# Attention probabilities turned by DMA instead of TensorE, with new order lists for every engine

## The chip, the cores and the metric

The kernel runs on one core of one Trainium2 chip. The metric is the device time of one execution in microseconds (us). Times of instructions come from one profiled execution. The engines are TensorE (PE for matmuls, PEld for its weight loads), VectorE (DVE), ScalarE (ACT), GpSimd (POOL) and SyncE (SP), whose queue here only issues DMAs.

## The reference

128 graphs of 128 nodes with 256 features. First one transformer layer (8 heads of 32), masked and biased by the adjacency matrix, then a stack of two layers of graph attention with one head:

```
nx = ln(x); q, k, v = nx@wq+bq, nx@wk+bk, nx@wv+bv                # 8 heads of 32
attn = softmax(q k^T / sqrt(32) + (0.1*adj*adj where adj > 0, else -inf))
x1 = x + (attn v)@wo + bo
x  = x1 + gelu(ln(x1)@w1+b1)@w2 + b2                              # hidden width 1024
for l in (0, 1):
    q, k = x@Wq[l].T + bq[l], x@Wk[l].T + bk[l]                   # width 128
    a = softmax(masked(q k^T / sqrt(128)))
    x = ln(x + (a x)@Wc[l].T)
```

## The kernel before

The graphs are taken in 32 groups of four (B = 4, NG = 32). A group passes through stages: N (first norm), Q (queries, keys, values), A (attention, output projection, second norm), M (the MLP), C0 and C1 (the two layers of graph attention). Each stage is cut into steps. `M.up3` is the fourth of eight chunks of the hidden layer; `A.exp2` is the exponential of the third graph's eight heads. Products in full precision are made of three float16 matmuls of high and low halves (`mm3`, lines 327 to 329), so nearly every operand is first split: ACT writes the high half, DVE or POOL the low half.

Nothing is scheduled while the kernel runs. Each engine has a list of steps written out by hand of a planner, `TENSOR`, `SCALAR`, `VECTOR`, `GPSIMD` and `SYNC`, which it goes through once in each iteration, and a second list (`..._END`) for the last. An entry as `A.exp2-1` means: in iteration n, step exp2 of stage A for group n-1. So groups overlap, five or six of them at a time, and each engine does its steps in exactly this order. Semaphores hold the engines together: `need(engine, signal, group, per, k)` waits for a count.

What the steps around the change do, for graph b of a group:

- `A.S` (PE, L1297) makes the scores of 8 heads in psA, two banks of PSUM. `A.S` on DVE (L872) scales them, adds the bias and writes `sc[:, b % 2]` (float32, in SBUF, inside the tile `area`). `A.max` (DVE, L877) takes the maxima.
- `A.exp` (ACT, L667) runs 8 exponentials over `sc`.
- `A.PT` (PE, L1304) transposes the 8 blocks of 128x128 float32 back into psA. ACT `A.PT` (L673) writes the high half of psA into `pT16`, DVE `A.PT` (L880) the low half.
- `A.AV` (PE) multiplies by v, 24 matmuls; DVE normalizes them into `o_rows`. After the fourth, `A.oT` splits `o_rows` (ACT L677 high, DVE L896 low), SP turns both halves by two DMA transposes into `rot_h`, `rot_l`; `A.wo` (PE) projects.
- DVE `A.wo` (L902) adds the residual, `A.st` (L749, L754) takes mean and variance, POOL `A.rs` (L544, L546) the inverse root, DVE `A.xh` (L762) normalizes, `A.mT` and `M.mT` split and turn again (ACT L681, DVE L913, SP), and `M.up0` to `M.up7` read the result.
- `M.up` on ACT is Gelu (L688) and a cast (L691), then DVE (even chunks) or POOL (odd chunks, L334) makes the low half, and `M.down` (PE) needs it. `psUp` is bank 3 of PSUM, and `psQ[1]`, into which `Q.q1`, `Q.k1` and `Q.v1` are made, is bank 3 too.
- Exp and Gelu need different function tables on ACT. A load of the table (`ACT_TABLE_LOAD`) stands wherever a step with Exp follows one with Gelu or the other way round; copies, casts and Identity need none.

The transposes of the other operands (xT, oT, mT, and xT of C0 and C1) are already done by SP's queue, two of 128x1024 float16 each, by `turn`:

Of the kernel before, what the change touches and what calls it, by code (L numbers as in the profile page):

```python
# [1395 lines left out]
```

## Time and profile before

| | |
|---|---|
| median of 3 runs | 2076.52 us (2076.26 to 2077.35) |
| the profiled execution | 2075.52 us |
| its span, first to last instruction | 2073.3 us |
| PE busy | 1868.7 us (90%) |
| DVE busy | 1701.3 us (82%) |
| ACT busy | 1563.1 us (75%) |
| POOL busy | 925.4 us (45%) |
| share of the 16 DMA engines, SP's queue | 38.6% |

Busy is the time in which an engine has an instruction under way. After some 110 us of filling, the kernel repeats itself once for each group until the last ones drain, so one such period shows nearly everything.

### The profile page before, as it was taken

To read this page: it belongs to the slowest core of one execution; us is meant where nothing else is said; L and a number is where in the kernel's file an instruction comes from. 1 tells how busy PE (TensorE), PEld (TensorE's weight loads), DVE (VectorE), ACT (ScalarE), POOL (GpSimd) and SP (SyncE) were. 2 spreads that over 40 slices of the span, in tenths; PEclk is the share of its full clock that TensorE was granted. 3 is DMA by queue.
4 is the path that set the end of the run, shared out by engine and by line. 5 is a ranking of instruction groups with operands and counts; after the bars stand their busy time and mean duration, and the time that the engine had idled before them with its cause. 6 is when DMAs were issued, how large, how long until landed. Compare 5 with 4: busy or idle time off the path is not lost.

```text
span 2073.3 us, 44187 instructions
## 1 busy us (share of the span) xinstructions
PE 1868.7 (90%) x15704; PEld 1347.0 (65%) x15704; DVE 1701.3 (82%) x3402; ACT 1563.1 (75%) x2996; POOL 925.4 (45%) x1168
## 2 busy tenths in 40 slices
PE   4688899999999999999999999999999999999886
PEld 3455566676666667666666766666676666666664
DVE  4766788888888888888888888888888888888756
ACT  2477677778877777887777788777778877777762
POOL 3021425555443555544355554435555443555445
PEclk8788899999999999999999999999999999999998
DMA  6212344433344443334444343444443344443212
GB/s 168 70 40 70 92 102 113 102 87 78 84 111 102 113 103 88 77 85 111 103 113 103 87 78 85 110 103 112 103 87 75 88 110 102 113 103 78 57 48 60
DMA packets 441657, 192.45 MB, mean 93 GB/s; under 512 B 347808, under 2 KB 416416, under 8 KB 441440
## 3 DMA queue, kind: packets, MB, share of 16 engines
q1 hardware_dynamic: 440416, 188.04, 38.6%
q8 instruction: 128, 2.10, 0.4%
q0 software_dynamic: 544, 0.80, 0.2%
q10 hardware_dynamic: 480, 0.79, 0.1%
q14 instruction: 89, 0.73, 0.1%
HBM read 38.55 MB, written 16.78 MB: 27 GB/s over the span
## 4 chain that ended last, share of the span: by engine, by line
PE 60%; ACT 18%; DVE 10%; POOL 5%; issue 4%; DMA 1%; SPq 1%; ACTq 0%; DVEq 0%; POOLq 0%
PE ps L327 16%; PE ps L329 16%; PE ps L328 16%; PE ps L1304 6%; ACT area L667 4%; PE ps L1366 3%; DVE st L749 2%; ACT L688 2%; DVE area L762 2%; ACT cs L709 2%; POOL hid_l L334 2%; DVE area L902 2%; ACT L709 2%; POOL rs L546 2%; POOL ve L544 2%
## 5 line engine op out<-in xcount | busy, mean ns | idle before, releaser
L544 POOL TENSOR_TENSOR ve<-mv,eps_cols 128x4 f32<-128x4 f32 x128 | 64.1, 500 | 738.5 <-DVE mv L754 738.5
L667 ACT ACTIVATE area<-area,nmax 128x128 f32<-128x128 f32 x1024 | 312.6, 390 | 17.0 <-DVE nmax L877 16.2
L327 PE MATMUL ps<-w_h,hid_h 128*128 128x256 f16 x1024 | 279.5, 273 | 12.1 <-POOL hid_l L334 12.1
L334 POOL TENSOR_TENSOR hid_l<-area,hid_h 128x512 f16<-128x512 f32 x128 | 156.4, 1222 | 279.1 <-ACT hid_h L691 279.1
L328 PE MATMUL ps<-w_l,hid_h 128*128 128x256 f16 x1024 | 279.3, 273 | 0.0
L329 PE MATMUL ps<-w_h,hid_l 128*128 128x256 f16 x1024 | 279.2, 273 | 0.0
L688 ACT ACTIVATE area<-ps,b_col 128x512 f32<-128x512 f32 x256 | 176.1, 688 | 41.0 <-PE ps L329 37.9
L327 PE MATMUL ps<-rot_h,w_h 128*128 128x512 f16 x512 | 198.5, 388 | 8.4 <-ACT area L688 5.3
L328 PE MATMUL ps<-rot_l,w_h 128*128 128x512 f16 x512 | 198.0, 387 | 0.0
L329 PE MATMUL ps<-rot_h,w_l 128*128 128x512 f16 x512 | 197.9, 387 | 0.0
L880 DVE SCALAR_TENSOR_TENSOR pT<-ps,pT 128x1024 f16<-128x1024 f32 x128 | 156.1, 1220 | 20.1 <-ACT pT L673 20.1
L551 POOL TENSOR_TENSOR x<-x,cb_row 128x256 f32<-128x256 f32 x240 | 167.3, 728 | 4.7
L858 DVE SCALAR_TENSOR_TENSOR qk<-ps,bqk_col,qk 128x512 f16<-128x512 f32 x128 | 95.6, 747 | 84.2 <-ACT qk L656 84.2
L691 ACT CAST hid_h<-area 128x512 f16<-128x512 f32 x256 | 158.2, 618 | 8.2
L872 DVE SCALAR_TENSOR_TENSOR area<-ps,biasA 128x1024 f32<-128x1024 f32 x128 | 154.9, 1211 | 5.3 <-PE ps L1297 5.3
L877 DVE TENSOR_REDUCE nmax<-area 128x8 f32<-128x1024 f32 x128 | 155.4, 1214 | 2.2
L673 ACT ACTIVATE pT<-ps 128x1024 f16<-128x1024 f32 x128 | 130.3, 1018 | 25.3 <-PE ps L1304 25.3
L1304 PE MATMUL ps<-ident,area 128*128 128x128 f32 x1024 | 138.3, 279 | 11.4 <-ACT area L667 6.7
L1366 PE MATMUL ps<-area,cs 128*128 128x256 f32 x512 | 125.2, 388 | 20.3 <-ACT cs L719 19.1
L1304 PEld LDWEIGHTS ps<-ident,area 128*128 128x128 f32 x1024 | 117.9, 144 | 33.6 <-issue 17.4
L697 ACT CAST sC_h<-area 128x1024 f16<-128x1024 f32 x32 | 33.4, 1045 | 137.8 <-DVE area L921 137.8
L546 POOL TENSOR_TENSOR rs<-ve,minus_half 128x4 f32<-128x4 f32 x128 | 132.7, 1036 | 10.0
(201 smaller groups left out, 5821.2 us busy)
## 6 DMA issues: line engine op xcount, KB each, us to landing
qkS<-qk SPq DMA_DIRECT2D x378, 128.0 KB, 2.3
xin<-in_x SPq DMA_DIRECT2D x32, 512.0 KB, 4.7
adj_in<-in_adj SPq DMA_DIRECT2D x64, 256.0 KB, 2.8
out<-x SPq DMA_DIRECT2D x30, 512.0 KB, 2.8
area<-in_L_gnn_w SPq DMA_DIRECT2D x1, 1024.0 KB, 7.9
area<-in_L_gnn_w SPq DMA_DIRECT2D x2, 512.0 KB, 9.2
rot_h<-sA_h SPq DMA_TRANSPOSE x64, 2.8
rot_l<-sA_l SPq DMA_TRANSPOSE x64, 2.7
```

Of the source, the lines that this page charges most:

```text
L327: pe.matmul(dst, lh, rh, start=start, stop=False, **kw)
L328: pe.matmul(dst, lh, rl, start=False, stop=False, **kw)
L329: return pe.matmul(dst, ll, rh, start=False, stop=stop, **kw)
L334: eng.tensor_tensor(hid_l[:, c % RING, :], hidden[:, c % 2, :], hid_h[:, c % RING, :], ALU.subtract).then_inc(done, 1)
L546: pool.tensor_tensor(rs[:, n], ve[:, n], minus_half[:, :], ALU.pow).then_inc(p_rs[n], 1)
L551: last = pool.tensor_tensor(dst[:, b], src[:, b], row, op)
L667: last = act.activation(sc[:, b % 2, h], sc[:, b % 2, h], ACT.Exp, bias=nmax[:, b, h:h + 1])
L688: act.activation(hidden[:, b % 2, :], psUp, ACT.Gelu, bias=b1_col[:, b:b + 1], scale=1.0 / W_SCALE).then_inc(a_gelu, 1)
L691: act.copy(hid_h[:, b % RING, :], hidden[:, b % 2, :]).then_inc(a_hi, 1)
L880: dve.scalar_tensor_tensor(pT16[:, b % 2, 1], psA_heads, P_SCALE, pT16[:, b % 2, 0], ALU.mult, ALU.subtract).then_inc(d_PT, 1)
L1304: last = pe.transpose(psA_heads[:, h], sc[:, b % 2, h], ident[:, :])
L1366: last = pe.matmul(rows_of(l, g)[:, b], cs[:, l, b], places(l, g)["cW"][:, b], start=True, stop=True)
```

## The change

The 8 transposes on PE are gone. ACT writes the high half of the probabilities straight from `sc` in SBUF into a new tile `sP_h`, DVE the low half into `sP_l`, both in the layout of `sc`, and SP turns each by one DMA transpose of 128x1024 float16 into `pT16`. There is one `sP_h` and one `sP_l`, so the splits of graph b wait until both transposes of graph b-1 have landed (`m_PT`). `sc[:, b % 2]` becomes free with the low half (`d_PT`) and no longer with the PE transposes. All ten order lists are new, and with them the waits on PE for banks that come free (`freed` and the `at ==` ladder). Two preparations in the first group move from `Q.mA` to `A.S0`.

```diff
+        sP_h, sP_l = sb("sP_h", [P, H, P], F16), sb("sP_l", [P, H, P], F16)
...
+                    elif what[:2] == "PT":
+                        b = int(what[2])
+
+                        need_apart(sp, t_AV, g, B, b - 1)
+                        need_apart(sp, a_PT, g, B, b + 1)
+                        sp.dma_start_transpose(pT16[:, b % 2, 0], sP_h.rearrange("p h k -> p (h k)"))\
+                            .then_inc(m_PT, 16)
+                        need_apart(sp, d_PT, g, B, b + 1)
+                        sp.dma_start_transpose(pT16[:, b % 2, 1], sP_l.rearrange("p h k -> p (h k)"))\
+                            .then_inc(m_PT, 16)
...
                     elif what[:2] == "PT" and stage == "A":
-                        need(act, t_PT, g, B, b + 1)
-                        need(act, t_AV, g, B, b - 1)
-                        act.activation(pT16[:, b % 2, 0], psA_heads, ACT.Copy, scale=P_SCALE).then_inc(a_PT, 1)
+                        need(act, a_exp, g, B, b + 1)
+                        need(act, m_PT, g, B * TURN, b * TURN)
+                        act.activation(sP_h[:, :, :], sc[:, b % 2], ACT.Copy, scale=P_SCALE).then_inc(a_PT, 1)
...
-                        need(dve, t_PT, g, B, b - 1)
+                        need(dve, d_PT, g, B, b - 1)
...
                         need(dve, a_PT, g, B, b + 1)
-                        dve.scalar_tensor_tensor(pT16[:, b % 2, 1], psA_heads, P_SCALE, pT16[:, b % 2, 0],
+                        need(dve, m_PT, g, B * TURN, b * TURN)
+                        dve.scalar_tensor_tensor(sP_l[:, :, :], sc[:, b % 2], P_SCALE, sP_h[:, :, :],
...
-                    elif stage == "A" and what[:2] == "PT":
-                        need(pe, a_exp, g, B, b + 1)
-                        for h in range(H):
-                            last = pe.transpose(psA_heads[:, h], sc[:, b % 2, h], ident[:, :])
-                        last.then_inc(t_PT, 1)
                     elif what[:2] == "AV":
-                        need(pe, d_PT, g, B, b + 1)
+                        need(pe, m_PT, g, B * TURN, (b + 1) * TURN)
```

Of the lists, the first line of ACT's before and of ACT's after:

```diff
-SCALAR = ["M.up2-2", "A.PT0-1", "M.up3-2", "A.exp1-1", "M.up4-2", "Q.k0+0", "A.PT1-1", "M.up5-2",
+SCALAR = ["M.up2-2", "A.exp1-1", "M.up3-2", "A.PT1-1", "M.up4-2", "Q.k0+0", "M.up5-2", "A.exp2-1",
```

From ACT's order in the middle of the program, before: the stretch of one iteration from `A.exp2` (L667) to `C0.ex` (L709), with `Q.q1`, `Q.k1` (L656), `C1.xT` (L697) and the high halves of graphs 2 and 3 (L673) between them.

```order
L667 ACT_TABLE_LOAD
L667 ACTIVATE area<-area,nmax 128x128 x8
L656 ACTIVATE qk<-ps,bqk_col 128x512
L697 CAST sC_h<-xh 128x1024
L673 ACTIVATE pT<-ps 128x1024
L667 ACTIVATE area<-area,nmax 128x128 x8
L656 ACTIVATE qk<-ps,bqk_col 128x512
L673 ACTIVATE pT<-ps 128x1024
L709 ACTIVATE cs,csum<-cs,cmax 128x128 x4
```

Of the changed kernel at the same place, from `A.exp3` (now L681) to `C0.ex` (L723) and on to `A.oT` (L691); the Gelu of `M.up6` is L702, its cast L705.

```order
L681 ACTIVATE area<-area,nmax 128x128 x8
L702 ACT_TABLE_LOAD
L702 ACTIVATE area<-ps,b_col 128x512
L705 CAST hid_h<-area 128x512
L687 ACTIVATE sP_h<-area 128x1024
L711 CAST sC_h<-xh 128x1024
L670 ACTIVATE qk<-ps,bqk_col 128x512
L723 ACT_TABLE_LOAD
L723 ACTIVATE cs,csum<-cs,cmax 128x128 x4
L670 ACTIVATE qk<-ps,bqk_col 128x512
L729 ACTIVATE area<-ps 128x1024
L691 CAST sA_h<-area 128x1024
```

`M.up6` stood ahead of the three exponentials and now stands among them, with a table load on either side. Over the whole program ACT has 191 table loads before and 249 after.

From SP's order, before: from the transposes of `N.xT` through the store to `C1.xT`, `A.oT` and the stacking copies `Q.stk` (L478).

```order
L429 DMA_TRANSPOSE xT_h<-sN_h 128x8x128
L432 DMA_TRANSPOSE xT_l<-sN_l 128x8x128
L496 DMA out<-x 128x4x256
L429 DMA_TRANSPOSE cT_h<-sC_h 128x8x128
L432 DMA_TRANSPOSE cT_l<-sC_l 128x8x128
L429 DMA_TRANSPOSE rot_h<-sA_h 128x8x128
L432 DMA_TRANSPOSE rot_l<-sA_l 128x8x128
L478 DMA qkS<-qk 32x2x1024 x12
```

Of the changed kernel, from the same `N.xT` on to `C1.xT`; of the pairs for graphs 0, 1 and 2 the last stands here, and the pair behind the store is graph 3's.

```order
L455 DMA_TRANSPOSE pT<-sP_h 128x8x128
L458 DMA_TRANSPOSE pT<-sP_l 128x8x128
L510 DMA out<-x 128x4x256
L455 DMA_TRANSPOSE pT<-sP_h 128x8x128
L458 DMA_TRANSPOSE pT<-sP_l 128x8x128
L433 DMA_TRANSPOSE cT_h<-sC_h 128x8x128
L436 DMA_TRANSPOSE cT_l<-sC_l 128x8x128
```

Eight transposes for each group are added to SP's queue between `N.xT` and `C1.xT`.

## Rows read from the trace of the kernel before

**Rows 1.** Stretches of one period: length, PE, PEld, DVE, ACT, POOL busy, PEclk, DMA share, GB/s.
```profile
1011.00:1054.60 43.60, 41.24 (x368) 28.83 (x366) 38.15 (x78) 41.38 (x86) 22.69 (x29) 1.00 0.25 62
1054.60:1063.40 8.80, 8.40 (x69) 7.09 (x67) 7.41 (x13) 4.16 (x5) 4.09 (x5) 1.00 0.87 178
1063.40:1071.40 8.00, 7.13 (x58) 5.25 (x57) 6.77 (x16) 2.97 (x4) 2.11 (x2) 1.00 0.76 202
sum 60.40, PE 56.77 PEld 41.17 DVE 52.33 ACT 48.51 POOL 28.88; mean PE 18.92 PEld 13.72 DVE 17.44 ACT 16.17 POOL 9.63
```

**Rows 2.** One tile, sA_h: the casts of M.mT, with their first and last start.
```profile
L681 ACT CAST sA_h<-area x32: 1044/1045/1047, 99.3 to 1975.4; 128x1024 f16<-128x1024 f32 x32
```

**Rows 3.** Waits of ACT from 1011 to 1054.6 us: total, times, longest.
```profile
ACT area L688 <- PE ps L329: 0.8, 2, 0.4
ACT pT L673 <- PE ps L1304: 0.7, 1, 0.7
ACT sA_h L677 <- DVE area L889: 0.3, 1, 0.3
```

**Rows 4.** The chain that ended last, through one period: start, duration, what.
```profile
1053.04 0.43 DVE area L889
1053.49 1.05 ACT sA_h L677
...
1057.85 1.35 POOL hid_l L334
...
1063.39 1.24 DVE area L902
...
1070.39 1.05 ACT sA_h L681
```

**Rows 5.** Groups of instructions by line: busy, mean ns; idle before.
```profile
L1304 PE MATMUL ps<-ident,area 128*128 128x128 f32 x1024 | 138.3, 279 | 11.4 <-ACT area L667 6.7 <-DVE area L872 3.8
L673 ACT ACTIVATE pT<-ps 128x1024 f16<-128x1024 f32 x128 | 130.3, 1018 | 25.3 <-PE ps L1304 25.3
L880 DVE SCALAR_TENSOR_TENSOR pT<-ps,pT 128x1024 f16<-128x1024 f32 x128 | 156.1, 1220 | 20.1 <-ACT pT L673 20.1
L853 DVE TENSOR_TENSOR sN_l<-area,sN_h 128x1024 f16<-128x1024 f32 x32 | 42.5, 1328 | 12.0 <-ACT sN_h L651 12.0
L607 ACT ACTIVATE w_h<-area 128x1024 f16<-128x1024 f32 x2 | 2.0, 1094 | 0.0
L688 ACT ACT_TABLE_LOAD x95 | 121.9, 1283 | 3.0 <-PE ps L329 1.0 <-DVE hid_l L334 0.3
```

**Rows 6.** ACT in order of time, late in the first stretch.
```profile
1043.47 0.67 ACT L656 ACTIVATE qk<-ps,bqk_col 128x512 f16<-128x512 f32 x1
1044.04 1.03 ACT L697 CAST sC_h<-xh 128x1024 f16<-128x1024 f32 x1
1044.98 1.02 ACT L673 ACTIVATE pT<-ps 128x1024 f16<-128x1024 f32 x1
1045.89 2.44 ACT L667 ACTIVATE area<-area,nmax 128x128 f32<-128x128 f32 x8
...
1050.50 0.39 ACT L709 ACTIVATE cs<-cs,cmax 128x128 f32<-128x128 f32 x1
```

**Rows 7.** The chain again: one matmul of 256 columns, one of 512.
```profile
1046.36 0.11 PE ps L327
...
1046.90 0.22 PE ps L328
```

**Rows 8.** PE in order of time: the first matmul of A.AV1 and the first behind it.
```profile
1044.61 0.18 PE L327 MATMUL ps<-v_h,pT 128*128 128x33 f16 x1
...
1045.22 0.27 PE L327 MATMUL ps<-w_h,hid_h 128*128 128x256 f16 x1
```

**Rows 9.** One tile, rot_h: SP's time to issue a transpose, and to landing.
```profile
L429 SPq DMA_TRANSPOSE rot_h<-sA_h x64: 1231/1274/1430, 83.9 to 1976.5; - x64
...
DMA to landing us min/median/max: 2.7/2.8/3.3
```

More of the change, by code:

```diff
@@ L75 @@
-QK = ("q0", "q1", "k0", "k1")
-TENSOR_END = ["M.down2-2", "C0.S-3", "A.AV0-1", "A.S3-1", "C0.xW-3", "A.PT2-1", "M.down3-2",
-              "M.up6-2", "A.AV1-1", "A.PT3-1", "A.AV2-1", "M.down4-2", "C0.PT-3", "A.AV3-1",
-              "M.up7-2", "M.down5-2", "M.down6-2", "C0.PV-3", "M.down7-2", "A.wo-1", "C1.k-4",
-              "C1.q-4", "C1.S-4", "C1.xW-4", "C1.PT-4", "M.up0-1", "C1.PV-4", "M.up1-1", "C0.q-2",
-              "M.up2-1", "M.down0-1", "M.up3-1", "C0.k-2", "M.up4-1", "M.down1-1", "C0.S-2",
-              "M.up5-1", "M.down2-1", "C0.xW-2", "M.up6-1", "M.down3-1", "C1.q-3", "C1.k-3",
-              "M.up7-1", "C1.S-3", "C0.PT-2", "M.down4-1", "M.down5-1", "C0.PV-2", "M.down6-1",
-              "C1.PT-3", "M.down7-1", "C1.xW-3", "C1.PV-3", "C0.q-1", "C0.k-1", "C0.S-1", "C0.xW-1",
-              "C0.PT-1", "C1.k-2", "C0.PV-1", "C1.q-2", "C1.S-2", "C1.xW-2", "C1.PT-2", "C1.PV-2",
-              "C1.k-1", "C1.q-1", "C1.S-1", "C1.xW-1", "C1.PT-1", "C1.PV-1"]
@@ L107 @@
-GPSIMD_END = ["C0.rs-3", "C1.rs-4", "M.lo1-1", "M.lo3-1", "C1.af-4", "M.lo5-1", "A.x1b-1",
-              "C0.af-3", "M.lo7-1", "C0.rs-2", "C1.rs-3", "C0.af-2", "C0.rs-1", "C0.af-1",
-              "C1.af-3", "C1.rs-2", "C1.af-2", "C1.af-1", "C1.rs-1"]
-SYNC_END = ["M.ldC-2", "A.oT-1", "C1.xT-4", "M.mT-1", "C0.xT-2", "C1.xT-3", "C1.sto-4", "M.ldC-1",
-            "C0.xT-1", "C1.xT-2", "C1.xT-1", "C1.sto-3", "C1.sto-2", "C1.sto-1"]
+TENSOR = ["M.up0-2", "C1.PV-5", "M.up1-2", "M.up2-2", "A.S2-1", "M.down0-2", "M.down1-2", "M.up3-2",
+          "Q.k0+0", "C0.q-3", "M.up4-2", "M.up5-2", "A.S3-1", "Q.q0+0", "C0.k-3", "M.up6-2",
+          "A.AV0-1", "M.down2-2", "C0.S-3", "A.AV1-1", "M.down3-2", "M.down4-2", "Q.q1+0",
+          "C0.xW-3", "Q.k1+0", "A.AV2-1", "M.down5-2", "A.AV3-1", "C0.PT-3", "M.up7-2", "M.down6-2",
+          "C0.PV-3", "Q.v1+0", "M.down7-2", "A.wo-1", "C1.k-4", "C1.q-4", "C1.S-4", "Q.v0+0",
+          "C1.xW-4", "A.S0+0", "A.S1+0", "C1.PT-4"]
@@ new lines @@
+QK = ("q0", "q1", "k0", "k1")
+TENSOR_END = ["M.up0-2", "C1.PV-5", "M.up1-2", "M.down0-2", "C0.k-3", "A.S2-1", "M.up2-2", "C0.q-3",
+              "M.up3-2", "A.S3-1", "M.down1-2", "C0.S-3", "M.down2-2", "A.AV0-1", "C0.xW-3",
+              "M.up4-2", "A.AV1-1", "M.down3-2", "M.up5-2", "M.up6-2", "A.AV2-1", "C0.PT-3",
+              "M.down4-2", "C1.q-4", "A.AV3-1", "M.up7-2", "M.down5-2", "C0.PV-3", "M.down6-2",
+              "M.down7-2", "C1.k-4", "A.wo-1", "C1.xW-4", "C1.S-4", "C1.k-3", "C1.PT-4", "C1.PV-4",
+              "M.up0-1", "C1.q-3", "C0.q-2", "M.up1-1", "M.down0-1", "M.up2-1", "C0.k-2", "M.up3-1",
+              "M.down1-1", "M.up4-1", "C0.S-2", "M.up5-1", "M.down2-1", "C1.S-3", "M.down3-1",
+              "M.up6-1", "C0.xW-2", "M.up7-1", "C0.PT-2", "M.down4-1", "C0.PV-2", "M.down5-1",
+              "M.down6-1", "M.down7-1", "C1.xW-3", "C1.PT-3", "C1.PV-3", "C0.q-1", "C0.k-1",
+              "C0.S-1", "C0.xW-1", "C1.k-2", "C0.PT-1", "C0.PV-1", "C1.q-2", "C1.S-2", "C1.xW-2",
+              "C1.PT-2", "C1.PV-2", "C1.k-1", "C1.q-1", "C1.S-1", "C1.xW-1", "C1.PT-1", "C1.PV-1"]
@@ new lines @@
+SCALAR_END = ["A.exp1-1", "M.up2-2", "A.PT1-1", "C0.q-3", "C0.k-3", "M.up3-2", "A.exp2-1",
[8 rows of a table added]
+VECTOR_END = ["A.max0-1", "A.S1-1", "M.mC-3", "C1.PV-5", "A.max1-1", "M.lo0-2", "A.PT0-1", "A.S2-1",
[10 rows of a table added]
+GPSIMD_END = ["C0.rs-3", "A.rs-1", "C1.rs-4", "M.lo1-1", "C1.af-4", "M.lo3-1", "M.lo5-1", "A.x1b-1",
+              "C0.af-3", "M.lo7-1", "C0.rs-2", "C1.rs-3", "C0.af-2", "C0.rs-1", "C0.af-1",
+              "C1.af-3", "C1.rs-2", "C1.af-2", "C1.rs-1", "C1.af-1"]
+SYNC_END = ["A.PT3-2", "C1.xT-5", "A.oT-2", "Q.stk-1", "M.mT-2", "M.ldC-3", "C0.xT-3", "A.PT0-1",
+            "A.PT1-1", "A.PT2-1", "C1.sto-5", "C1.xT-4", "A.PT3-1", "A.oT-1", "C1.xT-3", "M.mT-1",
+            "M.ldC-2", "C0.xT-2", "M.ldC-1", "C1.sto-4", "C0.xT-1", "C1.xT-2", "C1.xT-1",
+            "C1.sto-3", "C1.sto-2", "C1.sto-1"]
@@ L779, in prepare @@
                     prepped()
-                elif step == "Q.mA":
+                elif step == "A.S0":
                     lows(HALVES_QKV, HALVES_QKVO)
@@ L1127, in iteration @@
+                    if step == "M.up0":
                         freed(g, (d_v[1], -1, 1, 1), (a_gelu, 1, 8, 8))
```

252 lines of the change are left out of this document (125 added, 127 removed), and 51 rows, old and new, of tables (SCALAR, SCALAR_END, TENSOR, VECTOR).

## The prediction

> **What bounds the kernel now.** The page says PE 90% busy, DVE 82%, ACT 75%, and an average like that would make the PE transposes the thing to remove. So I first asked for the repeating period. The casts of M.mT start 32 times from 99.3 to 1975.4 us [rows 2], so a period is (1975.4 - 99.3) / 31 = 60.5 us. Then I followed the chain that ended last through one period. It leaves PE at two places: behind A.oT on ACT it goes over a table load, Gelu and cast of M.up7 to POOL's low half at 1057.85, then M.down7 and A.wo on PE; then DVE at 1063.39, over the norm's mean and root, and ACT again with the cast of M.mT at 1070.39 [rows 4].
>
> From that I cut the period at three events and asked for the busy time of each engine between them [rows 1]:
>
> - from the end of M.mT's cast on ACT to the end of A.oT's cast on ACT: 43.6 us, ACT busy 41.4, PE 41.2;
> - from there to the end of A.wo on PE: 8.8 us;
> - from there to the end of the next M.mT cast: 8.0 us, over DVE, POOL, DVE, ACT.
>
> These three add up to the period, 60.4 us, and they are a closed loop. The first stretch is ACT's own list, gone through in order; the other two are chains of dependent work in which neither PE's nor ACT's load matters. The reader is to see that ACT, idle 12 us in a period, is idle there almost only in the last two. In the first it waits 0.8 us for matmuls of M.up, 0.7 us for A.PT on PE and 0.3 us for the last A.AV [rows 3], together 1.8 us; the rest of the stretch is ACT instructions end to end. PE is nearly as full there, so both matter, but taking work off PE can win no more than those 1.8 us unless ACT's list gets shorter too.
>
> **The change part by part.** Per period:
>
> *PE.* Four groups of 8 transposes go. All 128 together are busy for 138 us [rows 5], 1.08 each, so PE's 56.8 us a period fall to about 52.5. On a kernel bound by PE alone this would be the gain. Here it reaches the loop only through ACT's 1.8 us.
>
> *ACT, what is the same.* Between the casts of M.mT and A.oT the new list has the same steps as the old but one: Q.v0, a cast of about 0.5 us (its neighbours of 512 columns follow each other at 0.57, from 1043.47 to 1044.04 [rows 6]), now stands ahead of M.mT, where ACT waits anyway. That takes 0.5 off the stretch.
>
> *ACT, table loads.* The old list changes between Exp and Gelu 5 times in this stretch, the new 7 times: loads ahead of C1.ex, M.up0, A.exp1, M.up3, A.exp2, M.up6 and C0.ex. One load takes 1283 ns [rows 5]. Two more are 2.6 us, and nothing hides them, because ACT has no idle time there. Over the program it is 249 loads for 191, 58 more, 74 us of ACT, which is 29 periods with two more each; the periods at the ends have fewer.
>
> *ACT, the high half.* It now reads float32 from SBUF and no longer from PSUM. From PSUM it takes 1018 ns; casts of the same size from SBUF take 1045 [rows 2], and a scaled copy from SBUF 1094 [rows 5]. So each costs between 0.03 and 0.08 us more, four of them 0.1 to 0.3; I take 0.3, since an instruction behind one from PSUM also starts early (0.91 us after it, from 1044.98 to 1045.89 [rows 6]).
>
> *DVE.* The low half takes 1220 ns from PSUM; a low half made wholly from SBUF takes up to 1328 [rows 5]. 0.4 us at most for a group, on an engine that is busy 52.3 of 60.4 us. That is hidden as long as the period stays above about 54.
>
> *DMA and SP.* Eight more transposes. SP takes 1.27 us to issue one and it lands 2.8 us from issue [rows 9], so SP is held 10.2 us more in a period. Issue by issue they stand behind N.xT and ahead of C1.xT. Pair by pair: the high half's is issued while DVE makes the low half (1.2 us), the low half's lands 2.8 us behind DVE. With one sP the next graph's split must wait 1.2 + 2.8 = 4.0 us from its cast, and between two such casts ACT now always has an exponential (2.44 us [rows 6]) and at least one M.up. For graph 3, the split stands right behind M.up6 on ACT, and A.AV3 on PE has Q.q1, C0.xW, Q.k1, A.AV2 and M.down5 ahead of it, 7 us, more than 4.0. So I cost the DMAs at nothing; if that cover were gone, each microsecond by which AV3 is late is one on the loop, since A.oT follows it. C1.xT's transposes queue behind graph 3's pair by at most 1.3 us, and C1.q is half a period away.
>
> *What is late next.* ACT's idle time in the stretch does not vanish wholly. Q.q1 writes bank 3, in which the Gelu of M.up6 reads, so the whole run from M.up6's Gelu to A.oT starts at once on both engines. On PE: Q.q1 6 x 0.22 = 1.3, C0.xW 24 x 0.11 = 2.6, Q.k1 1.3, A.AV2 0.6 [rows 8], M.down5 12 x 0.11 = 1.3, A.AV3 0.6, the last one's end a further 0.2 [rows 7], then 0.7 for DVE's reciprocal and its product (0.43 [rows 4]): 8.6 us. On ACT over the same run: cast 0.5, high half 1.0, C1.xT 0.94, Q.q1 0.57, load 1.3, C0.ex 4 x 0.39 = 1.6, Q.k1 0.57, C0.xW 0.9: 7.4 us [rows 5, 6]. ACT will wait 1.2 us for the last A.AV ahead of A.oT, where it waited 0.3. Of the 0.8 for M.up I leave 0.1, for PE has less before it. Idle: 1.3 us.
>
> *The sum.* The stretch is 43.6 - 1.8 - 0.5 + 2.6 + 0.3 + 1.3 = 45.5 us, the period 45.5 + 8.8 + 8.0 = 62.3 where it was 60.4. That is 1.9 us for each of 29 periods, 55 us. The profiled execution took 2075.5 us, so 2130.5; it is 1 us under the median of the runs shown, so 2131.
>
> For the bounds: with no idle at all and the high half at no more than before, the stretch is 43.9 and the period 0.3 us longer, 2085; with the 0.3 for the high half, 2094. With the 1.8 us of idle time all left and the 1.2 besides, the stretch is 44.2 + 3.0 = 47.2, +3.6 a period, 2180.
>
> **A rule against it.** The Trainium skill, in "ScalarE: Activation LUTs", section "Table sets: the hidden batching unit", says to batch calls by table set, and gives some 2.7 us for a load. The list of after goes against the rule. The trace agrees with the rule and not with that figure: 1283 ns [rows 5]. By the Trainium skill's figure the two loads would be 5.4 us a period and the estimate 2131 + 29 x 2.8 = 2212.
>
> **The rivals.**
>
> *PE's time comes back (10%).* If PE sets the period and ACT only follows it, the 128 transposes come off whole, 138 us, and the time is 1938. For it: PE 56.8 of 60.4 us busy, 41.2 of 43.6 in the first stretch. Against it: ACT has 41.4 there, and its list grows. It decides if ACT's stretch comes out under 43.6, which needs the two loads to fall into waiting time; I find only 1.8 + 0.5 us of that to spend against 2.9.
>
> *No change (4%).* The two effects cancel to within 0.14 us a period, 2076. This is also where it would end if the 58 loads sat in idle time and PE's relief went unused. A measurement here tells differences above about 0.2% (4 us) from none.
>
> *The transposes are late (11%).* SP issues in order. If its place in the list makes each low half wait (behind N.xT's, or for A.AV of two graphs before, whose pT16 it overwrites), A.AV3 slips and A.oT with it. For it: SP has no slack that I could read from a list, and the 16 DMA engines are 76 to 87% busy in the last two stretches [rows 1]. Against it: the first stretch, where most of the new ones fall, has 25%. Price: 1.5 us a period would be 44 us on top, 2175.
>
> *A DMA transpose at its price for one block (1%).* If a DMA turned its 8 blocks of 128x128 one after another at more than PE's whole A.PT each, the ring would need over 60 us a period for eight of them and set the time, far above 2200. The trace has 2.8 us for all 8 [rows 9], which nearly rules it out. The Trainium skill, "VectorE: DVE Perf Modes", section "The three transpose paths", has 1309 ns for a 128x128 block by DMA and 390 by TensorE and advises TensorE where PSUM is a possible destination. By it an estimate is 8 x 8 x 1.3 = 84 us a period and some 2760 us.
>
> **How the numbers follow.** The forecast, slower by the table loads, has 74%. Its own range is 2094 to 2150 for most of it. To hold the time 8 times in 10 I take 2088 (near the lower bound) to 2168 (part of the late transposes); the faster rival stays outside. Faster by over 0.2% 10%, within 0.2% 4%, slower 86% (74 + 11 + 1).
>
> **What the profile of after would show.** Right: a period near 62.3 us; ACT busy near 51 us in it and 43 to 44 of the stretch from M.mT's to A.oT's cast; 7 loads there at 1283 ns; PE busy about 52.5 a period with idle time where it now has none; a wait of about 1 us of the cast of A.oT for DVE; the other two stretches still 8.8 and 8.0. The first step is wrong if the stretch between the casts is under 43.6 us. The DMA step is wrong if PE's A.AV waits for pT. The forecast fails too if the granted clock of PE, 1.00 in all three stretches now, falls as PE idles more.

## The result

The kernel after takes 2168.41 us, median of 3 runs (2164.00 to 2172.01), where the kernel before takes 2076.52: 92 us more, a ratio of 1.0442 with a 95% interval of 1.0425 to 1.0458. The forecast was slower, at 2131 with a range of 2088 to 2168, and the measured time lies 0.4 us above its top. The sign came out as forecast, the size did not: 92 us against 55. How much of the forecast's mechanism stands is told below: two loops turned out to be nearly equally long.

The page of after, its engines and the groups of instructions that answer to [rows 5]. The columns are line, engine, operation, tiles, then busy us, mean ns of one, and the idle time before them with what ended it:

```profile
PE 1823.7 (84%) x14680; PEld 1245.6 (58%) x14680; DVE 1720.8 (79%) x3402; ACT 1641.3 (76%) x3054; POOL 1032.0 (48%) x1168
...
L338 POOL TENSOR_TENSOR hid_l<-area,hid_h 128x512 f16<-128x512 f32 x128 | 175.2, 1368 | 369.0 <-ACT hid_h L705 369.0
...
L895 DVE SCALAR_TENSOR_TENSOR sP_l<-area,sP_h 128x1024 f16<-128x1024 f32 x128 | 174.6, 1364 | 35.3 <-ACT sP_h L687 35.2
...
L702 ACT ACT_TABLE_LOAD x124 | 159.1, 1283 | 3.2 <-PE ps L333 1.0
...
L687 ACT ACTIVATE sP_h<-area 128x1024 f16<-128x1024 f32 x128 | 134.5, 1050 | 16.7 <-DMA pT<-sP_l 16.5
...
pT<-sP_h SPq DMA_TRANSPOSE x128, 2.7
pT<-sP_l SPq DMA_TRANSPOSE x128, 2.7
```

The reader is to see four things. PE has lost its transposes and is at 84% where it was at 90. ACT has 124 loads ahead of Gelu where it had 95 [rows 5]. The transposes land 2.7 us from issue, close to the 2.8 costed (a median; the longest of the low halves takes 4.9). And two groups are dearer than before though the same work: the low half on DVE, 1364 ns for 1220, and POOL's low half of hidden, 1368 ns for 1222 on the page of before.

The casts of M.mT in after, which answer to [rows 2]:

```profile
L695 ACT CAST sA_h<-area x32: 1044/1045/1046, 105.6 to 2075.6; 128x1024 f16<-128x1024 f32 x32
```

(2075.6 - 105.6) / 31 is a period of 63.55 us where it was 60.52: 3.03 us in each of 31 periods, 94 us, which is the whole loss. The same three stretches as in [rows 1] follow for a period of after that ACT's waits lengthen, and behind it the first stretch of a short period. Columns: stretch, length, then busy us of PE, PEld, DVE, ACT and POOL with their instructions, PEclk, DMA share, GB/s:

```profile
1060.13:1107.44 47.31, 39.95 (x338) 25.40 (x337) 40.34 (x72) 43.48 (x86) 25.38 (x27) 0.96 0.47 112
1107.44:1116.01 8.57, 8.49 (x69) 7.16 (x68) 6.63 (x18) 4.56 (x6) 5.07 (x7) 1.00 0.85 159
1116.01:1124.05 8.04, 7.21 (x54) 5.29 (x53) 6.78 (x16) 3.15 (x5) 2.10 (x2) 1.00 0.64 163
sum 63.92, PE 55.65 PEld 37.85 DVE 53.75 ACT 51.19 POOL 32.54; mean PE 18.55 PEld 12.62 DVE 17.92 ACT 17.06 POOL 10.85
...
997.62:1043.53 45.91, 39.39 (x338) 25.81 (x336) 38.82 (x72) 43.51 (x86) 25.18 (x27) 0.96 0.57 116
```

The second and third stretches are what they were. The first holds 43.5 us of ACT work, 2.1 more than before, in the short period as in the long one. It is 45.9 us long at its best, 0.4 above the 45.5 of the forecast, and 47.3 in the period shown. What fills the difference is waiting, ACT's waits in the long one (total, times, longest), which answer to [rows 3]:

```profile
ACT sA_h L691 <- DVE area L904: 1.3, 1, 1.3
ACT area L702 <- POOL hid_l L338: 1.1, 1, 1.1
ACT sP_h L687 <- DMA pT<-sP_l: 1.0, 1, 1.0
```

The first of them was forecast at 1.2. The other two were not: a Gelu that waits for POOL's low half two chunks before it, since the Gelu overwrites the half of `hidden` that POOL still reads, and a high half of the split that waits until the transposes of the graph before have left the one sP. Over 27 such periods the means are 1.5 us ahead of A.oT, 0.8 for POOL, 0.4 for sP and 0.2 for M.up, 3.0 us in all with the smallest ones, where the forecast had 1.3.

The last of the three waits is the rival of the late transposes in small. The chain that ended last goes over it in this period (start, duration, what):

```profile
1092.24 0.04 PE ps L333
...
1092.44 1.23 SPq L455
...
1093.78 4.24 DMA pT<-sP_l
...
1098.10 1.07 ACT sP_h L687
```

SP issues graph 2's pair only behind A.AV0 on PE, whose half of `pT16` it overwrites, and here the low half's transpose takes 4.24 us to land; then ACT goes on with graph 3's split.

The granted clock is at its lower level about once in each period. In the long period above it falls here, PE in order of time and then three windows around it:

```profile
1085.93 0.39 PE L331 MATMUL ps<-xT_h,wqk_h 128*128 128x512 f16 x1 [1.98 <-DVE qk L872]
1086.15 0.46 PE L332 MATMUL ps<-xT_l,wqk_h 128*128 128x512 f16 x1
1086.40 0.63 PE L333 MATMUL ps<-xT_h,wqk_l 128*128 128x512 f16 x1
```

```profile
1083.90:1085.90 2.00, 0.05 (x1) 0.00 (x0) 1.91 (x3) 1.49 (x3) 0.34 (x1) 1.00 0.58 131
1086.40:1089.70 3.30, 3.30 (x9) 1.22 (x8) 2.49 (x5) 3.29 (x10) 2.46 (x4) 0.50 0.02 5
1089.80:1093.10 3.30, 3.30 (x43) 2.25 (x42) 2.65 (x4) 3.30 (x8) 3.22 (x4) 1.00 0.01 2
```

PE has stood still for 1.98 us ahead of Q.q0, waiting for DVE's Q.k0. It starts again, and from 1086.4 to 1089.7 its clock is 0.50, the 1.2 GHz level: a matmul of 512 columns takes 0.43 us from start to start (1086.40 to 1086.83) where [rows 7] have 0.22. In other periods it falls behind a wait of 1.60 us ahead of A.S1. Before, the clock was 1.00 in all three stretches [rows 1].

### The profile page after: what moved, and what is told of

It is laid out like the page before. It is cut to its first block, busy times and chain, and to the rows that moved or that the text cites. A ratio compares the mean times of both kernels' runs of the same rounds, so it can differ in the third digit from the quotient of the medians.

```text
span 2166.3 us, 42837 instructions
## 1 busy us (share of the span) xinstructions
PE 1823.7 (84%) x14680; PEld 1245.6 (58%) x14680; DVE 1720.8 (79%) x3402; ACT 1641.3 (76%) x3054; POOL 1032.0 (48%) x1168
## 3 DMA queue, kind: packets, MB, share of 16 engines
q1 hardware_dynamic: 710752, 255.18, 52.5%
## 4 chain that ended last, share of the span: by engine, by line
PE 33%; DVE 29%; ACT 16%; issue 9%; POOL 7%; DMA 5%; SPq 1%; DVEq 0%; ACTq 0%; POOLq 0%
PE ps L331 11%; PE ps L333 10%; PE ps L332 10%; DVE st L763 4%; DVE area L776 3%; DMA pT<-sP_l 3%; DVE area L886 3%; POOL hid_l L338 3%; ACT area L702 3%; DVE sP_l L895 3%; DVE nmax L891 3%; ACT area L681 3%; POOL rs L560 2%; ACT L702 2%; DVE x L970 2%
## 5 line engine op out<-in xcount | busy, mean ns | idle before, releaser
L338 POOL TENSOR_TENSOR hid_l<-area,hid_h 128x512 f16<-128x512 f32 x128 | 175.2, 1368 | 369.0 <-ACT hid_h L705 369.0
L681 ACT ACTIVATE area<-area,nmax 128x128 f32<-128x128 f32 x1024 | 312.5, 390 | 16.6 <-DVE nmax L891 15.8
L331 PE MATMUL ps<-rot_h,w_h 128*128 128x512 f16 x512 | 208.4, 407 | 60.5 <-ACT area L702 57.4
L702 ACT ACTIVATE area<-ps,b_col 128x512 f32<-128x512 f32 x256 | 175.9, 687 | 46.5 <-PE ps L333 23.8
L332 PE MATMUL ps<-rot_l,w_h 128*128 128x512 f16 x512 | 206.7, 404 | 0.0
L895 DVE SCALAR_TENSOR_TENSOR sP_l<-area,sP_h 128x1024 f16<-128x1024 f32 x128 | 174.6, 1364 | 35.3 <-ACT sP_h L687 35.2
L565 POOL TENSOR_TENSOR x<-x,cb_row 128x256 f32<-128x256 f32 x240 | 195.3, 844 | 4.7
L886 DVE SCALAR_TENSOR_TENSOR area<-ps,biasA 128x1024 f32<-128x1024 f32 x128 | 155.5, 1215 | 44.1 <-PE ps L1324 37.2
L565 POOL TENSOR_TENSOR x<-xh,cg_row 128x256 f32<-128x256 f32 x120 | 140.1, 1196 | 80.1 <-DMA out<-x 80.1
L331 PE MATMUL ps<-xT_h,wqk_h 128*128 128x512 f16 x256 | 102.3, 400 | 81.2 <-DVE qk L872 78.5
L705 ACT CAST hid_h<-area 128x512 f16<-128x512 f32 x256 | 158.2, 618 | 8.4
L702 ACT ACT_TABLE_LOAD x124 | 159.1, 1283 | 3.2 <-PE ps L333 1.0
L1324 PE MATMUL ps<-qkS 96*128 96x128 f16 x1024 | 83.2, 227 | 82.6 <-DVE area L886 60.7
L687 ACT ACTIVATE sP_h<-area 128x1024 f16<-128x1024 f32 x128 | 134.5, 1050 | 16.7 <-DMA pT<-sP_l 16.5
L331 PEld LDWEIGHTS ps<-rot_h,w_h 128*128 128x128 f16 x512 | 52.3, 102 | 152.4 <-ACT area L702 106.6
```

The costliest lines, as they stand in the source:

```text
L331: pe.matmul(dst, lh, rh, start=start, stop=False, **kw)
L332: pe.matmul(dst, lh, rl, start=False, stop=False, **kw)
L338: eng.tensor_tensor(hid_l[:, c % RING, :], hidden[:, c % 2, :], hid_h[:, c % RING, :], ALU.subtract).then_inc(done, 1)
L565: last = pool.tensor_tensor(dst[:, b], src[:, b], row, op)
L681: last = act.activation(sc[:, b % 2, h], sc[:, b % 2, h], ACT.Exp, bias=nmax[:, b, h:h + 1])
L687: act.activation(sP_h[:, :, :], sc[:, b % 2], ACT.Copy, scale=P_SCALE).then_inc(a_PT, 1)
```

## The experiments

All periods below are cut as above, and the means are over the same 27 periods of a run, without the first and last ones. "Low clock" is the time per period in which the records show the 1.2 GHz level. Stretch 1 runs from the cast of M.mT to that of A.oT.

| kernel | time, us | period | stretch 1 | ACT busy in it | low clock |
|---|---|---|---|---|---|
| before | 2076.5 | 60.5 | 43.5 | 41.3 | 0.0 |
| after | 2168.4 | 63.6 | 46.9 | 43.5 | 3.9 |
| e1 transposes by DMA, old lists | 2423.7 | 72.2 | 54.0 | 41.3 | 11.4 |
| e12 the same, A.PT3 first on SP | 2206.3 | 64.5 | 47.5 | 41.3 | 4.3 |
| e15 the same, two sP | 2200.3 | 64.4 | 47.4 | 41.2 | 3.3 |
| e2 before, no Gelu | 2055.1 | 60.1 | 43.3 | 35.0 | 0.5 |
| e3 after, no Gelu | 2136.5 | 62.7 | 46.4 | 34.5 | 3.7 |
| e4 before, two more loads | 2168.4 | 63.5 | 46.5 | 44.0 | 0.8 |
| e5 after, PE filled | 2153.2 | 63.1 | 46.4 | 43.4 | 0.3 |
| e13 the same, four hidden | 2140.5 | 62.6 | 45.9 | 43.4 | 0.1 |
| e6 after, two sP | 2165.0 | 63.6 | 46.9 | 43.5 | 4.0 |
| e7 after, Q.k0 earlier | 2205.2 | 64.9 | 48.3 | 43.6 | 5.3 |
| e9 the same, PE filled | 2162.9 | 63.5 | 46.9 | 43.4 | 0.4 |
| e8 e7 without Gelu | 2104.4 | 61.5 | 45.1 | 34.4 | 3.3 |
| e10 e9 without Gelu | 2103.7 | 61.6 | 45.1 | 34.4 | 0.0 |
| e11 after, five loads | 2291.2 | 67.7 | 51.0 | 41.1 | 8.2 |
| e14 the same, two sP, four hidden, PE filled in two places | 2276.7 | 67.2 | 50.6 | 41.1 | 5.8 |

e2, e3, e4, e8, e10, e12, e14 and e15 are single runs; their differences below a few us are not read.

**The transposes alone.** The DMA transposes went into the kernel before, its lists for ACT, DVE and POOL kept, A.PT taken out of PE's and put into SP's:

```diff
-SYNC = ["C1.xT-4", "A.oT-1", "Q.stk+0", "M.ldC-2", "N.ld+1", "M.mT-1", "C0.xT-2", "Q.ldA+1",
-        "N.xT+1", "C1.sto-4"]
+SYNC = ["C1.xT-4", "A.PT3-1", "A.oT-1", "Q.stk+0", "M.ldC-2", "N.ld+1", "M.mT-1", "C0.xT-2", "Q.ldA+1",
+        "N.xT+1", "A.PT0+0", "A.PT1+0", "C1.sto-4", "A.PT2+0"]
```

> The splits in SBUF and the DMA transposes of the changed kernel, but with the order lists of before: A.PT taken out of PE's list and put into SP's (graphs 0, 1 and 2 behind N.xT, graph 3 ahead of A.oT), nothing else moved, 191 table loads as before. If ACT's list with its two more table loads is what made the change slower, the DMA path by itself costs nearly nothing: ACT's stretch from M.mT to A.oT keeps its 41.8 us of work, gains 0.3 for reading SBUF, loses the 0.7 us wait for PE's transposes; period 60.0 to 60.6 us, time 2060 to 2085 us. If the DMA path itself (late transposes, POOL slowed by DVE's reads of SBUF, the clock) is the cause, most of the 92 us comes back here: 2130 us or more. If PE were the bound, its 138 us would come off: about 1940 us.

Measured: 2423.7 us (2423.51 to 2425.12), ratio 1.168 (1.1661 to 1.17). Had ACT's list been the whole cause, the time would have been at most 2085; it is 340 us above that, in the range of the rival (the DMA path itself, 2130 or more). PE's waits over one period, from 1025 to 1097 us:

```profile
PE ps L328 <- DMA pT<-sP_l: 10.6, 2, 7.2
```

A.AV stands still twice a period for the low half's transpose, 10.6 us in all. SP's queue over that place, in order of time (each row is one issue):

```profile
1067.31 1.25 SPq L452 DMA_TRANSPOSE pT<-sP_h  x1
1068.66 1.24 SPq L455 DMA_TRANSPOSE pT<-sP_l  x1
1076.75 1.23 SPq L430 DMA_TRANSPOSE cT_h<-sC_h  x1
1078.09 1.24 SPq L433 DMA_TRANSPOSE cT_l<-sC_l  x1
1079.52 1.23 SPq L452 DMA_TRANSPOSE pT<-sP_h  x1
```

Between graph 2's pair and graph 3's stands C1.xT, and SP waits 6.8 us before it may issue that. A later run swaps the two names:

```diff
-SYNC = ["C1.xT-4", "A.PT3-1", "A.oT-1", "Q.stk+0", "M.ldC-2", "N.ld+1", "M.mT-1", "C0.xT-2", "Q.ldA+1",
+SYNC = ["A.PT3-1", "C1.xT-4", "A.oT-1", "Q.stk+0", "M.ldC-2", "N.ld+1", "M.mT-1", "C0.xT-2", "Q.ldA+1",
```

> DMA transposes with the lists of before (2424 us), and on SP's queue A.PT3 ahead of C1.xT. If C1.xT's place on SP made A.AV3 late, its wait of 5.3 us falls by 2.5 (two issues) and the time to 2340 to 2360. If it is the distance from exp to A.AV in the old lists of ACT and PE that is short, nothing changes: 2400 to 2430.

Measured: 2206.3 us, 217 less, far more than the two issues that I had priced; both theories missed. The low clock fell with it, from 11.4 to 4.3 us a period, so the 217 are the swap and what follows from it. PE's waits over one period of it, from 1015.3 to 1079.6 us:

```profile
PE ps L328 <- DMA pT<-sP_l: 3.5, 1, 3.5
```

What stands ahead in SP's queue had cost its own waiting time, 6.8 us, besides two issues. With that mended the old lists, with their five loads, still lose 4.0 us a period. So the new lists as a whole do buy something: 0.9 us a period, two loads paid included. A second buffer of the split was given to this kernel as well:

> DMA transposes with the old lists, A.PT3 ahead of C1.xT on SP (2206 us, period 64.5, ACT waiting 1.4 for the DMA of the split before and 1.2 and 2.6 for PE behind it), and with two buffers of sP. If the reuse of sP delays the whole run: 1.4 us a period less, 2160 to 2170. If PE's A.AV waits for the transposes anyway: within 10 us of 2206.

2200.3 us: within the 10 us of the rival. ACT's wait for sP is gone (1.4 us a period to nothing), its wait for PE behind it is 3.7 us where it was 2.6. PE's A.AV waits the same 3.5 us.

**The table loads.** Two loads more in before, by an Exp of 4 columns ahead of M.up6's Gelu, everything else unchanged:

```diff
+                        if what == "up6":
+                            act.activation(tiny[:, :], minus_half[:, :], ACT.Exp)
```

> The kernel before with one Exp of 4 elements on ACT between M.up5 and M.up6: two more table loads a period (251 for 191), no other change, PE's transposes still in. Theory of ACT's list: each load is on the loop, 2.6 us and 0.3 for the small instruction, 2.9 us for each of 29 periods, 84 us: about 2160 us. If PE sets the period, the loads take ACT's idle time: under 2100 us.

2168.4 us. This was forecast within 10 us. Two loads in that stretch cost the kernel before 3.0 us a period: 2.7 more of ACT's work, the small Exp included, and 0.2 more of waiting for M.up. That it is also the time of after is a coincidence: there the loads are one term beside others, a cast less in the stretch, longer waits and the clock. Then the loads were taken out of both kernels, by Identity in place of Gelu:

> The kernel before with Identity in place of Gelu, so that ACT never changes its table (1 load for 191); this leaves out the Gelu. Theory of ACT's list: 5 loads leave the first stretch and 1 the second, 7.7 us of the 60.4 us period, until PE (56.8 us busy) holds it: period 57 to 58 us, 1970 to 2010 us.

> The changed kernel with Identity in place of Gelu (1 load for 249); this leaves out the Gelu. Theory of ACT's list: 8 loads go, 10.3 us of the 63.6 us period, until PE (52.5) or DVE (about 54) holds it: period 55 to 57 us, 1910 to 1970 us, so that the changed kernel is now the faster of the two. If the DMA path itself is the cause, it stays slower than the kernel before without loads by much of the 92 us: 2050 us or more.

2055.1 and 2136.5 us. The theory of ACT's list missed both by 45 us or more, in the same way: 6.3 and 9.0 us of ACT work left stretch 1, and it became 0.2 and 0.6 us shorter. The price of a load is one-sided in these kernels. A load added costs in full, a load taken away gives nearly nothing, so another engine's list is as long as ACT's.

The two runs say more, and it bears on the forecast. Without any load the changed kernel is still 81 us slower than the old one (2136.5 against 2055.1), which is the range that the second expectation gave to its rival (2050 or more). Of the 92 us no more than 32 go away with all the loads. So the two new loads are not the loss by themselves; in after the other loop alone, its low clock included, holds 62.7 us a period.

**Which list that is.** In after, PE's run to A.AV3 begins with Q.q0, and Q.q0 waits for Q.k0 on DVE (the 1.98 us above). In this kernel Q.k0 goes ahead of A.S3 on DVE:

```diff
-          "A.PT1-1", "A.S3-1", "Q.k0+0", "C1.xh-5", "M.lo4-2", "A.max3-1", "Q.q0+0", "A.PT2-1",
+          "A.PT1-1", "Q.k0+0", "A.S3-1", "C1.xh-5", "M.lo4-2", "A.max3-1", "Q.q0+0", "A.PT2-1",
```

> The changed kernel with one swap in DVE's list: Q.k0 ahead of A.S3. PE's Q.q0 waits 2.0 us for Q.k0's low half to leave bank 2, and DVE itself waits 0.75 us for PE's A.S3 ahead of it. With Gelu left out the changed kernel still took 2136 us, so a second loop, DVE's list from M.mT to Q.k0 and then PE's list from Q.q0 to A.AV3, is nearly as long as ACT's. If both loops are about equally long, shortening this one by up to 2 us gives back only the difference to ACT's: 0.3 to 1.2 us a period, 2133 to 2160 us. If this loop alone sets the period: 1.9 us a period, about 2112 us. If ACT's alone: no change.

> The same swap with Identity in place of Gelu (this leaves out the Gelu), so that both loops are shorter. If the loop over DVE and PE is what holds the changed kernel without loads at 62.7 us a period, the swap takes 1.5 to 2 us off each: 2075 to 2095 us, where the one without the swap took 2136. If something else holds it, the time stays near 2136 us.

2205.2 us with Gelu (2194.31 to 2205.89, ratio 1.0613, 1.0587 to 1.0638), 37 slower than after. All three theories missed: they had 8 to 35 faster, 56 faster, and no change. Without Gelu 2104.4, 32 faster than e3 where 41 to 61 were expected. The low clock rose to 5.3 us a period, and the periods without any were 62.52 to 62.54 us, as long as the best of after. To tell the swap from the clock, both were run with PE kept busy (the edit is that of e5, below):

> The kernel after with Q.k0 ahead of A.S3 on DVE, as in the run before this one, and with dummy matmuls of PE in the three places where it idles (ahead of A.S1, C1.PT and Q.q0). Theory: the loss of that swap, 2205 against 2168 us, was the clock alone, since its periods without a stretch at the lower level were 62.5 us; with PE kept busy all periods are 62.5 and the time is 2135 to 2153. Rival: the swap itself is late for A.S3 and so for the exponentials; then the time stays above 2165.

> The kernel of the run before with Identity in place of Gelu (the Gelu is left out), so that no table is loaded; 2104 us without the dummy matmuls. Theory of a second loop (DVE's list up to Q.k0, then PE's run to A.AV3) that is nearly as long as ACT's and is lengthened by the clock: without loads, with the swap and without low clock the period falls to 60.5 or below, 2060 to 2090. If the clock plays no part in that loop: 2100 to 2110.

2162.9 us (2159.57 to 2164.58, ratio 1.0414, 1.0396 to 1.0431) with Gelu: 42 of the us were the clock's, but 10 us more than e5 are the swap's own, between what the two theories said. Without Gelu 2103.7, the same as e8, though the low clock went from 3.3 us to nothing: there the clock is not on the path. The chain that ended last in e10 says what is:

```profile
1028.75 1.23 DVE area L886
1030.00 1.22 DVE nmax L891
1031.22 1.32 DVE st L763 x4
...
1038.29 1.14 DVE sN_l L867
1039.42 1.13 DVE nmax L891
1040.55 1.67 DVE sP_l L895
1042.34 1.23 DVE area L886
...
1044.22 1.67 DVE x L970 x4
1045.93 0.39 PE ps L331
```

M.mT's cast ends at 1027.6; from there the chain runs 18 us along DVE's list, and PE's run goes on from its end. (x4 is four pieces of one line put together.) This is the second loop: DVE's list up to the middle of stretch 1, then PE's run to A.AV3. It is about as long as ACT's, and so the table loads of after are only part of what holds it.

The chains of the other traces agree. Of stretch 1, over the same 27 periods, the chain that ended last lies to 80% on PE and 17% on ACT in before; to 34% on DVE, 32% on PE and 13% on ACT in after; to 50% on ACT in e4 and 51% in e13 (below). In before ACT's list and PE's tied, which is why the kernel pays in full for two loads more and gains only 0.4 us a period from six fewer (e2). No run has the new lists with the transposes still on PE, so what the lists cost and what the DMA path costs under them is not told apart.

**The clock.** Dummy matmuls of 512 columns stand in the three places where PE idles in after; their results are written over before anything reads them:

```diff
+            FILL = {"A.S1": (3, 7), "C1.PT": (3, 3), "Q.q0": (7, 8)}
...
+                    if step in FILL and 3 <= number(g) < NG - 3:
+                        bank, times = FILL[step]
+                        for _ in range(times):
+                            pe.matmul(ps[:, bank, :], w1_h[:, 0, 0:P], w1_h[:, 0, 0:R], start=True, stop=True)
```

> The changed kernel with matmuls of 512 columns that nobody reads put where PE idles: 7 ahead of A.S1 and 3 ahead of C1.PT into bank 3, 8 ahead of Q.q0 into bank 7, groups 3 to 28. In the changed kernel the granted clock is at its lower level for 3.9 us of each 63.6 us period, once behind A.S1 or once behind Q.q0. If those episodes follow PE's idle time and cost 0.5 to 1.3 us each time they fall in ACT's stretch, they vanish here and the time falls by 10 to 35 us, to 2133 to 2158 us. If the clock costs nothing, the time stays at 2168 or rises by what the extra matmuls delay.

2153.2 us (2151.58 to 2157.19), ratio 1.0372 (1.0355 to 1.0389). More work on PE makes the kernel 15 us faster: the low clock falls from 3.9 us a period to 0.3, and 0.5 us a period is what it had cost.

**One sP or two.** For the rival that the transposes are late:

```diff
-        sP_h, sP_l = sb("sP_h", [P, H, P], F16), sb("sP_l", [P, H, P], F16)
+        sP_h, sP_l = sb("sP_h", [P, 2, H, P], F16), sb("sP_l", [P, 2, H, P], F16)
```

> The changed kernel with two sP_h and two sP_l in turn (and a semaphore for each), so that a split no longer waits for the transposes of the graph before. ACT waits for them 0.40 us a period in the changed kernel. Theory of ACT's list: at most 0.4 us for each of 29 periods comes back, 0 to 12 us, 2156 to 2168 us. If late transposes are the main cost (1.5 us a period or more), 2125 us or less.

2165.0 us (2157.68 to 2173.61), ratio 1.0433 (1.04 to 1.0466). The median is 3 us below after's, and the ranges of the two overlap. The wait for the DMA is gone from ACT's list and the period is the same 63.6: the 0.4 us a period went into the waits behind it (A.oT from 1.5 to 1.7, a cast of Q from 0.1 to 0.3). Taking that wait away gave nothing that these runs can tell, although in the long period above the chain ran over it: what comes next is about as late.

**POOL's low half.** The Gelu's wait was taken away by its cause, with four buffers of hidden in place of two, in the kernel with PE filled:

```diff
-        hidden = area[:, 7168:8192].rearrange("p (s n) -> p s n", s=2)
+        hidden = sb("hidden4", [P, 4, R])
...
-                        need(act, (d_lo, p_lo)[b % 2], g, FC // 2, b // 2)
+                        need(act, (d_lo, p_lo)[b % 2], g, FC // 2, b // 2 - 1)
```

> The kernel after with PE's idle time filled (2153 us) and with four buffers of hidden in place of two, so that no Gelu waits for the low half of two chunks before, on POOL or DVE. If POOL's slower low half is on the loop: 0.8 us a period less, period 62.2, 2125 to 2135. If the wait only moves to the cast of A.oT (PE's run sets the end): 2146 to 2156, with that wait at 2.0 to 2.3 in place of 1.5.

2140.5 us (2139.03 to 2144.56), ratio 1.0307 (1.029 to 1.0324), 13 us less than e5 and 5 more than the first theory's band; the rival's is 6 away, and its sign is absent, for the cast of A.oT still waits 1.5 us. POOL's low half of M.up3 is as slow as before (2.1 us); only nobody waits for it. That slowness is half of the cause. The other half is ACT's new order: before, A.exp1 and its loads stood between M.up3 and M.up5 and now they do not. In e12, with the old lists and reads from SBUF, POOL's low half of M.up5 takes 2.1 us in 27 of 28 periods, and no Gelu waits for it. One period of it, in the columns of the windows above:

```profile
1049.80:1095.40 45.60, 42.13 (x356) 26.45 (x355) 39.81 (x72) 43.35 (x87) 25.80 (x27) 1.00 0.49 115
1095.40:1103.98 8.58, 8.49 (x70) 7.24 (x68) 6.63 (x17) 4.57 (x7) 5.07 (x7) 1.00 0.84 161
1103.98:1112.05 8.07, 7.25 (x55) 5.28 (x53) 6.79 (x16) 3.18 (x5) 2.10 (x2) 1.00 0.63 163
```

ACT's waits in the first of these stretches:

```profile
ACT sA_h L691 <- DVE area L904: 1.5, 1, 1.5
...
ACT hidden L702 <- PE ps L333: 0.3, 1, 0.3
```

Half of its periods are this one, 62.21 to 62.24 us: 43.4 of ACT, 1.5 ahead of A.oT, 0.3 for M.up and what lies between instructions. That is the forecast's sum (62.3), in the kernel from which the clock and POOL's wait are taken away. In part it is luck: ACT's work grew by 2.1 and not 2.4 us, the waits came to 1.8 and not 1.3, and stretches two and three are 0.15 us shorter than was put in.

**Five loads.** Last, the loads were cut by order. M.up6 goes ahead of the third exponential on ACT and PE, so that ACT's stretch has five loads as before:

```diff
-SCALAR = ["M.up2-2", "A.exp1-1", "M.up3-2", "A.PT1-1", "M.up4-2", "Q.k0+0", "M.up5-2", "A.exp2-1",
-          "Q.q0+0", "A.PT2-1", "C0.k-3", "C0.q-3", "A.exp3-1", "M.up6-2", "A.PT3-1", "C1.xT-4",
+SCALAR = ["M.up2-2", "A.exp1-1", "M.up3-2", "A.PT1-1", "M.up4-2", "Q.k0+0", "M.up5-2", "C0.q-3", "C0.k-3", "M.up6-2",
+          "A.exp2-1", "Q.q0+0", "A.PT2-1", "A.exp3-1", "A.PT3-1", "C1.xT-4",
```

> The kernel after with M.up6 moved ahead of the third exponential on ACT and PE (M.down2 goes ahead of it on PE, M.lo4 ahead of C1.xh on DVE), so that ACT loads five tables in the first stretch and not seven, and 191 or so in all. Theory that the loads set the stretch: 2.6 us less, of which up to 1.4 may be lost to waiting for M.lo4; period 1.2 to 2.6 shorter, 2090 to 2130. Theory that the second loop is as long as ACT's: less than 0.6 us a period, 2150 to 2170.

> The kernel with five loads (2291 us) and with two buffers of sP, four of hidden, and PE filled ahead of A.S1 and C1.PT. There the wait for the DMA transposes was 3.5 us a period and the low clock 8.2. If the one sP is what the two loads of the new lists pay for: both go, period 62 to 63, 2115 to 2150. If the run from the split over the DMA to A.AV3 is itself too long: the wait moves to the cast of A.oT and the time stays above 2200.

2291.2 us (2284.59 to 2297.56), ratio 1.1037 (1.1012 to 1.1062), outside both theories, and 2276.7 with the second sP, the four hidden and the fill. The second is above the 2200 of its rival, but the wait did not move to the cast of A.oT as the rival said. What I had read as a wait for the DMA (3.5 us a period) turned into a wait of Q.q0's cast for PE. Waits from 1048 to 1190 us, two periods, in e11 and then in e14:

```profile
PE ps L331 <- DVE qk L872: 10.5, 2, 5.3
...
ACT sP_h L687 <- DMA pT<-sP_l: 7.9, 2, 4.3
```

```profile
PE ps L331 <- DVE qk L872: 10.5, 2, 5.3
...
ACT qk L670 <- PE ps L333: 10.0, 4, 3.7
```

On ACT the cast of Q.q0 now stands behind M.up6 and an exponential, DVE's Q.q0 follows it, and A.AV0 on PE cannot start until DVE has read that bank: 5.3 us of PE in every period. So this order saves 2.4 us on ACT and loses more on PE. It says nothing for or against the price of a load. No kernel with the DMA transposes that computes the Gelu comes near the 2076.5 of before.

## Why the prediction had the sign right and the size too small

The step that failed is the idle time left to ACT in the first stretch, 1.3 us in the sum, with DVE's reads from SBUF called hidden and the clock put at nothing. ACT waits 3.0 us there on average, the stretch is 46.9 us for the forecast's 45.5, and the period 63.6 for 62.3. Keeping PE busy brings 15 us back (e5), and taking POOL's wait away 13 more (e13). Besides, the premise that ACT's list alone sets the stretch was half of the truth.

- **The loop of three stretches and ACT's list.** The three stretches are right: two and three kept their lengths (8.6 and 8.0 for 8.8 and 8.0), the loss lies in the first, and PE's 4.3 us a period came back nowhere. Even PE's busy time fell only from 56.8 to 55.7 us a period, where 52.5 was forecast; in part that is the low clock, the rest stays open. That ACT's list sets the first stretch holds when ACT gets more work (e4), not when it gets less (e2, e3).
- **ACT's terms.** Two loads, the moved cast and the SBUF read were summed to +2.4 us a period; ACT's busy time in the stretch rose by 2.2. e4 shows too that the kernel before pays for two loads in full. In after their price could not be isolated: e3 takes all loads out and gives 32 us, and e11 takes two out and opens another wait.
- **Idle left.** This is the term that was mis-sized: 1.3 us in the sum, 3.0 measured. 1.2 ahead of A.oT's cast was 1.5, and 0.1 for M.up was 0.2; nothing was put down for POOL's low half (0.8) and for sP (0.4).
- **DVE's low half "hidden".** On DVE it costs about what was said, 0.14 us each where 0.1 was allowed. But while it runs, POOL beside it takes up to twice as long, and on POOL's low half of M.up3 waits the Gelu of M.up5, which the new order has brought nearer. e13 puts the price of that wait at 13 us.
- **The clock.** Named as what would make the forecast fail, and costed at nothing. e5 puts it at 15 us. PE's new idle time was taken as free: without the transposes and under the new lists PE waits 1.98 us ahead of Q.q0 and 1.60 us ahead of A.S1, and the matmuls that follow one or the other run at half speed for 3.4 us.
- **The number of periods.** 29 were counted; the casts give 31 of 3.03 us each. At 1.9 a period that is another 4 us.
- **DMA and SP at nothing.** Right for the lists of after as far as e6 can tell: two sP change nothing clear of its scatter, and over the whole trace of after PE waits 2.7 us, in 7 times, for the low half's transpose. The cover of ACT's next split was less sure than argued: 16.5 us in 14 waits. It was not right as a statement on the transposes: under the lists of before they cost 347 us, of which 217 are SP's order. The rival "the transposes are late" describes e1 and e12; in after it shows only in the wait of the long period above, and its price there is within the scatter of e6.
- **The sum, put together again.** e13 has neither the wait for POOL nor, nearly, the low clock: 2140.5, 64 us over before. The wait for POOL adds 12.6 and the clock 15.2, taken away in this order; together 92. Of the 64, 31 periods at 62.2 for 60.5 make 53, near the forecast's 55; that does not show that the loads are these 53, since the second loop is nearly as long. The remaining 11 are periods of e13 that are longer than its best, most by up to 0.9 us. In the one whose waits I compared (from 1174.3) the cast of A.oT waits 2.0 us and not 1.5, and PE's A.AV 0.4 for pT; why some periods run so and others do not stays open.
- **The price of one load.** The prediction cites the Trainium skill, "ScalarE: Activation LUTs", section "Table sets: the hidden batching unit". Every load of after is again 1283 ns, 124 of them ahead of Gelu, and not some 2.7 us; in e4 two of them with the small Exp cost 3.0 us a period, so nothing near 2.7 for each appears in the time either. Its rule against alternating is borne out for the loads added (e4). e11, which removed loads by order, says nothing on it, for its order opened another wait.
- **What I had not seen at all** is that a second loop, over DVE and PE, is as long as ACT's. In before it was PE's list, in after it is DVE's list and PE's run. It would have held the kernel some 60 us above before (e3, 2136.5) had the loads cost nothing, so the forecast of a slower kernel did not rest on the loads alone, as its argument said; that is luck. It is also why e2 and e3 missed. My estimates of what ACT wins by having no loads (66 to 106 us in e2, 198 to 258 in e3) were three to eight times too high.

## What to carry to other kernels

When an engine that is nearly full is relieved in a schedule where another list closes the loop, the time can go up. Sum the other list first, and then look at what the relieved engine does in its new gaps, because here gaps of 1.6 to 2.0 us on TensorE were followed by 3.4 us at half its clock. A price read from one list held in one direction only: adding to the list that binds cost in full (e4), and taking from it gave back no more than the distance to the next loop (e2, e3). When a transfer moves to an in-order queue, what stands ahead of it there costs its own waiting time besides its issue time: two names swapped in SP's list were worth 217 us.
